# A recommendation tower on one core: seventeen tables picked by matmul instead of fifteen, sixty gathers instead of sixty-eight, and every dot product behind the last pick

## The reference

```
e = stack([tbl_f[ids[:, f]] for f in 0..31], axis=1)        # 512 x 32 x 128
dot = einsum('bnd,bmd->bnm', e, e);  z = dot[:, upper triangle without diagonal]   # 512 x 496
h = relu(concat([z, dense_ctx]) @ W_top1 + b_top1)           # 512 -> 512
h = relu(h @ W_top2 + b_top2)                                # 512 -> 256
y = h @ W_top3                                               # 256 -> 1
```

## Time and profile before

| what | value |
|---|---|
| median of three runs | 125.05 us |
| the three runs | 123.99, 125.05, 187.84 us |
| profiled execution, span (no other time of it is recorded) | 148.7 us |
| mean granted TensorE clock of it | 0.919 |
| PE, weight load, DVE, ACT, POOL busy | 82%, 67%, 51%, 53%, 48% |
| HBM read, written | 17.54 MB, 2.13 MB |

### The profile page before, as it was taken

One profiled execution on the slowest core, in us unless ns is written; L12 is line 12 of the kernel. 1 busy time (PEld: TensorE's weight loads), 2 busy tenths in 40 slices (PEclk: granted clock), 3 DMA queues, 4 the chain that ended last, 5 costly groups with the idle time before them and its releaser, 6 DMA issues.

```text
span 148.7 us, 2677 instructions
## 1 busy us (share of the span) xinstructions
PE 121.4 (82%) x1028; PEld 99.5 (67%) x1028; DVE 75.2 (51%) x196; ACT 78.8 (53%) x79; POOL 71.3 (48%) x76
## 2 busy tenths in 40 slices
PE   5889979989999689499995464321999899999993
PEld 3457758868788468378884452111999798999971
DVE  2999999989897399496800000000333033223301
ACT  3588899999997897799950510000143302210022
POOL 3877749787787477378775577772000000000000
PEclk9999999999999999959999776555599999999999
DMA  5998736666667356793221011211056441024000
GB/s 144 275 338 267 234 100 204 204 216 225 217 219 235 110 178 195 232 324 113 55 53 52 23 53 53 53 53 35 4 146 202 136 126 35 4 78 127 10 0 1
DMA packets 11150, 19.81 MB, mean 133 GB/s; under 512 B 2353, under 2 KB 7473, under 8 KB 11138
## 3 DMA queue, kind: packets, MB, share of 16 engines
q1 hardware_dynamic: 7522, 13.74, 29.8%
q0 software_dynamic: 2176, 4.46, 10.3%
q10 hardware_dynamic: 1440, 1.44, 3.0%
HBM read 17.54 MB, written 2.13 MB: 132 GB/s over the span
## 4 chain that ended last, share of the span: by engine, by line
PE 64%; ACT 15%; issue 11%; another core or an unknown queue 5%; DVE 2%; DMA 2%; ACTq 0%
PE two_ps L564 15%; PE two_ps L566 14%; PE two_ps L606 8%; PE two_ps L625 8%; ACT onehot L442 8%; PE free_ps L606 7%; ACT emb L421 5%; PE free_ps L636 3%; PE turn_ps L574 3%; PE two_ps L636 2%; ACT high L421 2%; DMA id_sb<-row_ids 2%; PE two_ps L641 1%; PE turn_ps L625 1%
## 5 line engine op out<-in xcount | busy, mean ns | idle before, releaser
L307 POOL DMA_INDIRECT rows<-tables,row_no x64 | 66.6, 1040 | 26.5 <-issue 14.9
L564 PE MATMUL two_ps<-onehot,high 128*128 128x512 f32 x128 | 52.7, 412 | 7.4 <-ACT onehot L442 4.3
L566 PE MATMUL two_ps<-onehot,low 128*128 128x512 f32 x128 | 50.9, 397 | 0.0
L442 ACT ACTIVATE onehot<-narrow 128x2560 fp32r<-128x2560 f16 (+3 forms) x16 | 35.5, 2226 | 4.8 <-PE two_ps L566 3.0
L564 PEld LDWEIGHTS two_ps<-onehot,high 128*128 128x128 f32 x128 | 24.8, 193 | 16.7 <-issue 10.4
L566 PEld LDWEIGHTS two_ps<-onehot,low 128*128 128x128 f32 x128 | 24.8, 194 | 4.7
L326 DVE TENSOR_SCALAR onehot<-pick_id,own_row 128x512 fp32r<-128x512 int16 x53 | 23.0, 479 | 4.4 <-PE two_ps L566 3.5
L316 DVE TENSOR_TENSOR low<-home,high 128x512 fp32r<-128x512 f32 (+1 forms) x36 | 22.4, 625 | 3.8 <-issue 3.7
L336 DVE TENSOR_SCALAR narrow<-pick_id,own_row 128x512 f16<-128x512 int16 x75 | 22.4, 365 | 0.0
L606 PE MATMUL two_ps<-emb 128*64 128x64 f32 x240 | 12.9, 247 | 9.4 <-issue 9.3
L196 DVE COPY home<-free_ps 128x512 f32<-128x512 f32 x4 | 2.8, 692 | 33.8 <-remote 29.8
(11 more groups left out here) (37 smaller groups left out, 54.5 us busy)
## 6 DMA issues: line engine op xcount, KB each, us to landing
home<-picked SPq DMA_DIRECT2D x10, 512.0 KB, 3.6
home<-picked SPq DMA_DIRECT2D x4, 640.0 KB
pick_id<-pick_ids SPq DMA_DIRECT2D x13, 128.0 KB, 3.7
w_sb<-w SPq DMA_DIRECT2D x3, 512.0 KB
dot_out<-home SPq DMA_DIRECT2D x10, 128.0 KB, 2.4
rows<-tables,row_no POOLq DMA_INDIRECT x64
dot_out<-home ACTq DMA_DIRECT2D x6, 128.0 KB, 2.6
pairs<-dot_out SPq DMA_DIRECT2D x10, 64.0 KB, 2.0
```

What stands on the lines that cost most here:

```text
L307: pool.indirect_dma_start(rows[:, k % ROWS_HELD, i, :], None, lone if one_table else tables, bass.IndirectOffsetOnAxis(ap=id_sb[:, 0, c:c ...
L442: act.activation(onehot[:, at:at + n, :], narrow[:, t % 2, n0:n0 + n, :], ACT.Copy).then_inc(onehot_act, n)
L564: pe.matmul(out, high[:, at, D * k:D * (k + 1)], onehot[:, c % HOT, :], start=(k == 0), stop=False)
L566: pe.matmul(out, low[:, at, D * k:D * (k + 1)], onehot[:, c % HOT, :], start=False, stop=(k == KR[t] - 1)).then_inc(picked_done, 1)
```

## The change

The list of picked tables grows to 17 (eleven of 8 chunks and six of 10: 148 chunks), so 15 tables are gathered, with 60 gathers. A gather now takes one feature of 128 samples from that feature's own table by the raw id; the joined table, `lone`, `row_no` and DVE's addition are gone. A block has four banks of 4, 4, 4 and 3 gathers, and all are turned and copied alike. PE turns 15 of the 16 banks among the picks, the last one after dot group 0; all eight groups then follow one another, then `layer1` of blocks 0 to 2 in one piece. The halved last bank, the halved last dots and their DVE copies are gone.

```diff
-PICK = 15
+PICK = 17
-BY_ACT = [2, 4, 5, 5, 5, 5, 5, 5, 5, 5, 5, 6, 6, 6, 6]
+BY_ACT = [2, 4, 5, 5, 5, 5, 5, 5, 5, 5, 5, 6, 6, 6, 6, 6, 6]
-TB, SUB = 4, 32
-MORE = GF - 4 * TB
-BANKS = 1 + BLK // SUB
+TB = 4
+BANKS = -(-GF // TB)
-TILES = [TB if k % BANKS else MORE for k in range(NB)]
+TILES = [min(TB, GF - TB * (k % BANKS)) for k in range(NB)]
-TURNED = PICK - 1
+TURNED = PICK - LAG
 def pace(c):
-    return min(51 * c // 20 - 10, CHUNK0[PICK])
+    return min(12 * c // 5 - 10, CHUNK0[PICK])
...
 # SP, block_out(r)
-                sp.wait_ge(dots_act, 2 * r + 2 + (r == LAST))
+                sp.wait_ge(dots_act, 2 * r + 2)
...
 # POOL
-                if k == 1:
-                    pool.wait_ge(row_no_ready, 1)
...
-                    one_table = k % BANKS == 0
                     pool.indirect_dma_start(
-                        rows[:, k % ROWS_HELD, i, :], None, lone if one_table else tables,
-                        bass.IndirectOffsetOnAxis(ap=id_sb[:, 0, c:c + 1] if one_table else row_no[:, c:c + 1], axis=0)
-                    ).then_inc(late_rows_in if k == NB - 1 and i >= TB // 2 else rows_in[k % ROWS_HELD], 16)
+                        rows[:, k % ROWS_HELD, i, :], None, tables[TB * (k % BANKS) + i],
+                        bass.IndirectOffsetOnAxis(ap=id_sb[:, c:c + 1], axis=0)
+                    ).then_inc(rows_in[k % ROWS_HELD], 16)
...
 # DVE
-            dve.wait_ge(row_ids_in, 16)
-            dve.tensor_tensor(row_no[:, :], id_sb[:, 0, :], id_sb[:, 1, :].bitcast(f32), ALU.add).then_inc(row_no_ready, 1)
...
-            for grp in range(GROUPS - 2):
+            for grp in range(GROUPS):
                 dots_out(grp)
-            relu1(0)
-            relu1(1)
-            dots_out(GROUPS - 2)
...
+            for r in range(LAST):
+                relu1(r)
 # ACT, emb_out(k)
-                if u == 0:
-                    out = emb[:, BLK * r:BLK * (r + 1), 4 * TB:GF]
-                    in_ = turn_ps[k % 2][:, 0:MORE * P].rearrange("p (f b) -> p b f", f=MORE)
-                else:
-                    b0 = BLK * r + SUB * (u - 1)
-                    out = emb[:, b0:b0 + SUB, 0:4 * TB].rearrange("p b (i f) -> p i b f", i=TB)
-                    in_ = turn_ps[k % 2][:, :].rearrange("p (i b f) -> p i b f", i=TB, f=4)
-                copy(out, in_).then_inc(emb_ready, 1)
+                copy(emb[:, BLK * r:BLK * (r + 1), TB * u:TB * u + TILES[k]],
+                     turn_ps[k % 2][:, 0:TILES[k] * P].rearrange("p (f b) -> p b f", f=TILES[k])).then_inc(emb_ready, 1)
...
 # PE, dot(grp, j)
-                r, half = divmod(2 * grp + j, BANKS - 1)
-                pe.wait_ge(emb_ready, BANKS * r + half + 2)
+                if grp % 2 == 0 and j == 0:
+                    pe.wait_ge(emb_ready, BANKS * (grp // 2 + 1))
...
 # PE, behind the loop of picks
-            turn(TURNED - 1)
-            pe.wait_ge(pick_emb_ready, TWOS + 1)
+            pe.wait_ge(pick_emb_ready, PICK - TWOS + 2)
             dot_group(0)
             turn(TURNED)
-            dot_group(1)
...
-            last_turn(0)
...
+            for grp in range(1, GROUPS):
+                dot_group(grp)
             pe.wait_ge(weights_in, 64)
...
+            for r in range(LAST):
+                if r == 2:
+                    pe.wait_ge(h1_dve, 1)
+                layer1(r)
```

More of the change, by code:

```diff
@@ L77, with build @@
 PARTS = [(0, 2), (2, 3), (3, 4)]
-def build(nc, row_ids, pick_ids, tables, lone, picked, context, w1, w2, small, y):
+def build(nc, row_ids, pick_ids, picked, context, w1, w2, small, tables, y):
     f32, f32r, i32, i16 = mybir.dt.float32, mybir.dt.float32r, mybir.dt.int32, mybir.dt.int16
@@ L95, in build @@
         ident = sb("ident", [P, P], f32)
-        id_sb = sb("id_sb", [P, 2, TILE0[NB]], i32)
-        row_no = sb("row_no", [P, TILE0[NB]], i32)
+        id_sb = sb("id_sb", [P, TILE0[NB]], i32)
         rows = sb("rows", [P, ROWS_HELD, TB, D], f32)
@@ L138, in build @@
         y_ps = [pick_ps[0][0:1, 0:2 * BLK], pick_ps[0][0:1, 2 * BLK:3 * BLK], pick_ps[1][0:1, 0:BLK]]
-        last_dot_ps = [dot_ps[1][1], dot_ps[0][1]]
         LAST = BLOCKS - 1
@@ L151, in build @@
         rows_in = [sem(f"rows_in{i}") for i in range(ROWS_HELD)]
-        late_rows_in = sem("late_rows_in")
         stored = sem("stored")
@@ L156, in build @@
         own_row_ready = sem("own_row_ready")
-        row_no_ready = sem("row_no_ready")
         high_ready = sem("high_ready")
@@ L166, in build @@
         emb_ready = sem("emb_ready")
-        last_emb_dve = sem("last_emb_dve")
         dots = sem("dots")
@@ L213, in y_out @@
                         sums.rearrange("p (r s g) -> p r s g", r=r1 - r0, s=4))
[L215 to L225, removed]
         block = ctx.enter_context(nc.Block())
@@ L242, in table_load @@
                              ).then_inc(table_in[t], 16)
-            sp.dma_start(id_sb[:, :, :], row_ids).then_inc(row_ids_in, 16)
+            sp.dma_start(id_sb[:, :], row_ids).then_inc(row_ids_in, 16)
             first = picked[0:P * KR[0], :].rearrange("(p k) d -> p (k d)", k=KR[0])
@@ L506, in half_in @@
                     pairs_load(act, r, q)
-            emb_out(TURNED - 1)
             dots_out(0)
+            emb_out(TURNED)
             dots_out(1)
             half_out(0)
-            emb_out(TURNED)
             dots_out(2)
@@ L515, in _ @@
             half_in(0)
-            for k in range(TURNED + 1, NB - 5):
-                emb_out(k)
             half_out(1)
@@ L520, in _ @@
             dots_out(5)
-            emb_out(NB - 5)
-            emb_out(NB - 4)
             half_in(1)
             dots_out(6)
-            emb_out(NB - 3)
-            emb_out(NB - 2)
             dots_out(7)
[L528 to L538, removed]
+            half_out(LAST)
+            half_in(LAST)
             for n in (0, 2):
@@ L607, in dot_pairs @@
                 last.then_inc(dots, 1)
[L609 to L617, removed]
             def dot_group(grp):
@@ L652, in _ @@
                     turn(t - LAG)
-            turn(TURNED - 1)
-            pe.wait_ge(pick_emb_ready, TWOS + 1)
+            pe.wait_ge(pick_emb_ready, PICK - TWOS + 2)
             dot_group(0)
             turn(TURNED)
-            dot_group(1)
[L658 to L666, removed]
-            pe.wait_ge(weights_in, 64)
[L668 to L673, removed]
-            last_turn(0)
[L675 to L683, removed]
+            for grp in range(1, GROUPS):
+                dot_group(grp)
+            pe.wait_ge(weights_in, 64)
+            for r in range(LAST):
+                if r == 2:
+                    pe.wait_ge(h1_dve, 1)
+                layer1(r)
             pe.wait_ge(h1_dve, 2)
@@ L697, in _ @@
             pe.wait_ge(dots_dve, GROUPS)
-            pe.wait_ge(dots_act, GROUPS + 1)
+            pe.wait_ge(dots_act, GROUPS)
             for n in range(N1):
@@ L722, in layout @@
     tbl = [np.asarray(inputs[f"tbl_{f}"]) for f in range(F)]
[L723 to L735, removed]
+    row_ids = ids[:, GATHERED].reshape(BLOCKS, BLK, GF).transpose(1, 0, 2).reshape(BLK, BLOCKS * GF)
     order = np.arange(B).reshape(BLOCKS, BLK // 4, 4).transpose(0, 2, 1).reshape(B)
@@ L757, in layout @@
             np.ascontiguousarray(ids[:, PICKED].T).view(np.int16)[:, ::2], (P, PICK, B))),
-        "tables": np.concatenate([tbl[f] for f in GATHERED[:4 * TB]]),
-        "lone": tbl[GATHERED[4 * TB]],
         "picked": np.concatenate([np.pad(tbl[f], ((0, P * k - ROWS[f]), (0, 0))) for f, k in zip(PICKED, KR)]),
@@ L764, in layout @@
         "small": np.ascontiguousarray(small),
+        **{f"table{f}": tbl[f] for f in GATHERED},
     }
@@ L775 @@
     y = nc.dram_tensor("y", (B, 1), mybir.dt.float32, kind="ExternalOutput").ap()
-    build(nc, *aps, y)
+    build(nc, *aps[:-GF], aps[-GF:], y)
     return run_bass_kernel_spmd(nc, [arrays], core_ids=[0]).results[0]["y"]
```

## The result

The changed kernel takes 132.52 us (median; 131.52 to 132.91) against 124.61 us for the kernel before: 1.0596 times as long, 95% interval 1.0538 to 1.0653. The forecast was 131.5, within 126.5 to 135.5; the difference is 7.9 us where 6.5 was forecast.

What follows compares the result with a forecast made beforehand. Without the pause, PE was taken as the bound from the first pick to the end. +9.3 + 1.3 - 2.0 - 2.1 = +6.5 us on the median of 125.05 gave 131.5 us, within 126.5 to 135.5.

Steps and rivals of the forecast that it cites:

- The pause set aside: 22.4 us lost around the first dot groups and before them, taken as absent from timed runs; span without it 126.3.
- the waits and the half clock that the rival had listed there: Among the picks: waits of 1.48 and 2.25 us and some 2 us around them, possibly missing from timed runs.
- Two more tables and 14 transposes, +9.3 and +1.3: PE's picks: two 10-chunk tables at 4.64 us each, +9.3; 14 more transposes among the picks at 0.09 each, +1.3.
- ACT sets the pace: Rival, in the picks: ACT's 5.7 us per 10-chunk table against PE's 5.0 adds +2.8, giving 134.3; chance 0.16.
- The rule of 131 ns per matmul: Skill figure for the added picks: 40 matmuls take 5.2 us, sum below 127.4; rejected for the row's 232 ns.
- Dots in one piece and transposes behind the picks, -2.0 and -2.1: Behind the picks: 18 fewer transposes, -2.0; two waits for bank copies and the split dot pieces go, -2.1.
- I take zero for these waits: New PE waits among dot groups and layers, for ACT's copies and `pairs`: counted as zero, bounds 0 and 1.5 us.
- a margin of 0.8: Before `layer1` of block 2: its `pairs` land at T + 21.8, needed at T + 22.6, T being group 0's start.
- one of the prediction's own signs of being wrong: At `layer1` of block 2: the forecast is wrong if block 2's `pairs` come late; no size given.
- The gathers: End of picks: 57th leaves POOL by 87.2, wanted at 90.0, 2.8 us to land; rival of late gathers 135, chance 0.06.
- The pause as a gain of the change: Rival, at dots beside gathers: usual runs hold up to 4.65 us of pause, which the change removes, 126.9; chance 0.20.

Runs made afterwards that it cites:

- the second trace of the kernel before: The kernel before, unchanged, run and profiled once more: 124.87 us, ratio 0.9999.
- With PE relieved of 4.6 us: The changed kernel with the second (low part) matmul of the last two picked tables left out, 20 matmuls: 129.86 us, ratio 1.0366.
- both traces of the changed kernel: The changed kernel's first profile (132.52 us) and the same kernel, unchanged, run once more beside later experiments: 132.83 us.
- the shared: The changed kernel with block 2's transfers split between SP and ACT: 132.07 us, ratio 1.0558.

## Why the prediction was right, and where a term was mis-sized

- **The pause set aside.** Right: the second trace of the kernel before has none, and 126.3 us, the span less the pause, compares with 123.0 us measured. The 3.3 us between lie among the picks, which end at 79.22 in the first trace and at 75.48 in the second; the waits and the half clock that the rival had listed there are not in the second at that size. One slip did no harm to the sum: spans were set against times, and a time is 1.8 us longer than its span.
- **Two more tables and 14 transposes, +9.3 and +1.3.** Right in sum: 10.4 measured for 10.6. But the reason given, that PE alone sets this, holds only half: ACT was right behind. With PE relieved of 4.6 us the picks ended 0.7 earlier; of the rest PE waited 2.1 for ACT, and 1.6 went to the lower clock. The rival "ACT sets the pace" named the next wait; its price of +2.8 did not come. The rule of 131 ns per matmul, set against the row, falls again: the Trainium skill, "TensorE: Matmul & The Clock Gate", section "Back-to-back issue gap", would have put the picks' end 6.5 us later (5.2 + 1.3), 3.9 less than measured.
- **Dots in one piece and transposes behind the picks, -2.0 and -2.1.** This is the term that was mis-sized: 2.5 measured for 4.1. The step that failed is "I take zero for these waits". Of its bounds, 0 to 1.5, 1.3 came as the wait for block 2's `pairs`, for which I had worked out a margin of 0.8. Two parts of it were too short: SP came to block 2's stores 1.7 us later than worked out, because block 1 took 4.8 us to land, and from these stores to the end of issuing the loads it took 7.1 us instead of the 5.3 of an undisturbed stretch. PE itself came 1.2 us late to `layer1(2)`, which hid part of it. The eight groups took 16.4 us with three transposes where 15.3 was worked out; groups 5 and 7 took 2.2 each instead of 1.87, with no wait named in the rows, so about 2.0 us came in all, above the upper bound. That block 2's `pairs` come late is one of the prediction's own signs of being wrong, and it came; it concerns this term and not the tables, which carry the result.
- **The number.** 131.5 and 132.5 are nearer than 6.5 and 7.9, because the kernel before came out at 124.61 instead of 125.05; that part is luck.
- **The gathers.** In time in both traces of the changed kernel. At the end of the picks the margin was 3.3 us behind the landing, more than worked out, since POOL never waited longer than 0.3 us between two gathers; in the middle of the picks, which I had not looked at, the shared and the sixteen-table kernels waited 0.3 to 1.1 us for rows at a turn. Beside DVE a gather took up to 1.4 us of POOL in the changed kernel, against 0.94 with DVE idle; it did not reach the path there.
- **The pause as a gain of the change.** Fell: there was nothing to give back.

## What to carry to other kernels

Moving work from one engine's list to another's is paid where the receiver is on the path: here 40 matmuls on a PE that was busy 92% of the span, in exchange for eight gathers whose end nobody waited for. Work that is packed into one piece brings its follow-up transfers closer together, so a transfer must be costed from when its queue will come to it, behind the transfers before it, and not by its old row alone. And when one trace is far longer than the timed runs, look for the stretch that holds the difference before reading any bound off it. The same holds for an experiment: look at the granted clock of its trace before what an edit gave back is read off it.

## What the runs showed of the hardware that was not expected

ACT's copy of two picked tables into `emb` writes pairs of neighbouring numbers, and it takes either 1.1 or 2.0 us, turn by turn. ACT in order of time, first in the kernel before, where the first pair starts at column 17 of 32, then in the changed kernel, where it starts at column 15:

```profile
19.45 1.10 ACT L421 ACTIVATE emb<-two_ps 128x1024 f32<-128x1024 f32 x1
...
26.97 2.01 ACT L421 ACTIVATE emb<-two_ps 128x1024 f32<-128x1024 f32 x1
```

```profile
20.08 1.96 ACT L392 ACTIVATE emb<-two_ps 128x1024 f32<-128x1024 f32 x1
...
28.68 1.11 ACT L392 ACTIVATE emb<-two_ps 128x1024 f32<-128x1024 f32 x1
```

The slow ones are at columns 19 (before) and 15 (after), byte 76 and 60, so that a pair of four-byte numbers lies across a multiple of 16 bytes; at column 17, byte 68, it does not. The Trainium skill, "SBUF — State Buffer", section "Specifications (TRN2)", gives SBUF 16-byte cachelines and a penalty for each crossing to a new one. The traces agree, and put the price at 0.9 us per copy of 512 pairs. The run with sixteen picked tables bears it out: there the pairs start at even columns, 16 the first, so none lies across, and all six copies take 1.10 to 1.23 us. The first two:

```profile
20.12 1.10 ACT L392 ACTIVATE emb<-two_ps 128x1024 f32<-128x1024 f32 x1
...
27.94 1.11 ACT L392 ACTIVATE emb<-two_ps 128x1024 f32<-128x1024 f32 x1
```

That run also has a table fewer; no run moved the columns alone, and what even columns would be worth at seventeen tables, where four of seven copies are slow, was not tried.
